# Six instead of four slots for the streamed activations, and all resident loads on one queue, in a fused attention and MLP kernel

## What is computed

```python
xn = layernorm(x)                                    # over the last axis, no gain or bias
w_masked = weight * block_mask(mask)                 # [4096, 4096], a block counts if its sum > 0
s = einsum('bsk,nk->bsn', xn, w_masked)
g = einsum('th,ih->ti', xn, w_gate) * s_gate         # 11008 wide
u = einsum('th,ih->ti', xn, w_up) * s_up
h = silu(g) * u
o = einsum('ti,hi->th', h, w_down) * s_down          # back to 4096
out = x + s * silu(o)
```

## Time and profile before

| | |
|---|---|
| two timed runs | 4385.27 and 4656.97 us, median 4521.12 |
| the profiled execution | 4384.07 us |
| its span on the slowest core, core 3 | 4382.5 us |
| spans of the other cores | 4360.7 to 4380.1 us |
| PE busy | 4082.6 us (93%) |
| DVE, ACT, POOL busy | 692.5, 210.4, 238.7 us |
| DMA, mean of the span | 137 GB/s |
| gate and up matmuls, L507 | 2,406 us |
| down matmuls, L681 | 728.0 us on `hTr`, 585.0 us on `hTl` |

### The profile page before, as it was taken

The page is one execution under the profiler, slowest core; times in us unless marked ns, Lnnn a source line. Parts: engine busy times, 40 slices in busy tenths (PEclk is TensorE's granted clock), DMA queues, the critical chain, the costliest instruction groups (busy, mean ns, idle before and its releaser), DMA issues. The chain is left out here.

```text
span 4382.5 us, 43424 instructions; the slowest of 8 cores (4360.7 to 4382.5 us)
## 1 busy us (share of the span) xinstructions
PE 4082.6 (93%) x19043; PEld 1849.6 (42%) x19043; DVE 692.5 (16%) x572; ACT 210.4 (5%) x265; POOL 238.7 (5%) x384
## 2 busy tenths in 40 slices
PE   1199998999999999999999999999499999999998
PEld 1144443444444444444444444444244444444443
DVE  4577631000000000000000000000000000000000
ACT  4100000000000000000000000000000000000000
POOL 0000000000000000000000000000011111111110
PEclk8599999999999999999999999999799999999999
DMA  4699643444444444444444444443778888887885
GB/s 155 239 336 333 245 154 72 85 85 86 86 87 87 87 87 87 87 87 87 87 87 87 87 87 87 87 87 77 204 155 180 194 177 163 194 192 157 184 194 133
DMA packets 205544, 599.18 MB, mean 137 GB/s; under 512 B 13156, under 2 KB 101552, under 8 KB 174000
## 3 DMA queue, kind: packets, MB, share of 16 engines
q0 software_dynamic: 120256, 287.33, 37.8%
q1 hardware_dynamic: 59808, 246.67, 16.9%
q10 hardware_dynamic: 25296, 62.40, 4.0%
HBM read 810.79 MB, written 47.71 MB: 196 GB/s over the span
## 5 line engine op out<-in xcount | busy, mean ns | idle before, releaser
L507 PE MATMUL p_g<-xnT,wgb 128*128 128x512 bf16 x5504 | 1204.3, 380 | 19.9 <-DMA wub<-hwu 19.9
L507 PE MATMUL p_u<-xnT,wub 128*128 128x512 bf16 x5504 | 1202.0, 379 | 0.0
L507 PEld LDWEIGHTS p_g<-xnT,wgb 128*128 128x128 bf16 x5504 | 539.9, 98 | 670.4 <-issue 23.4
L507 PEld LDWEIGHTS p_u<-xnT,wub 128*128 128x128 bf16 x5504 | 537.7, 98 | 650.2
L681 PE MATMUL p_acc<-hTr,wdb 128*128 128x512 bf16 x3072 | 728.0, 381 | 40.4 <-DMA hTr<-hTd 24.7
L681 PE MATMUL p_acc<-hTl,wdb 128*128 128x512 bf16 x2432 | 585.0, 384 | 30.3 <-DMA hTl<-hTd 30.3
L681 PEld LDWEIGHTS p_acc<-hTr,wdb 128*128 128x128 bf16 x3072 | 301.1, 98 | 417.5 <-issue 63.3
L542 DVE TENSOR_SCALAR uss<-p_u,su_cols 128x512 f32<-128x512 f32 x172 | 121.2, 746 | 2162.7 <-PE p_u L507 2162.7
L374 PE MATMUL p_sT<-xnT,wtm 128*128 128x512 bf16 x2048 | 448.6, 381 | 6.3 <-DVE wtm L425 6.3
L681 PEld LDWEIGHTS p_acc<-hTl,wdb 128*128 128x128 bf16 x2432 | 240.4, 99 | 325.2 <-issue 44.8
L374 PEld LDWEIGHTS p_sT<-xnT,wtm 128*128 128x128 bf16 x2048 | 199.1, 98 | 244.4 <-issue 9.5
(11 more groups left out here) (44 smaller groups left out, 302.7 us busy)
## 6 DMA issues: line engine op xcount, KB each, us to landing
wgb<-hwg POOLq DMA_DIRECT2D x86, 1024.0 KB, 8.7
wub<-hwu POOLq DMA_DIRECT2D x86, 1024.0 KB, 13.5
wdb<-hwd POOLq DMA_DIRECT2D x168, 512.0 KB, 6.9
hTl<-hTd SPq DMA_DIRECT2D x152, 512.0 KB, 5.5
mk<-mask SPq DMA_DIRECT2D x32, 2048.0 KB, 14.4
wts<-hwt SPq DMA_DIRECT2D x32, 2048.0 KB, 13.6
hTd<-hTt ACTq DMA_DIRECT2D x86, 256.0 KB, 10.2
xTl<-xT SPq DMA_DIRECT2D x32, 512.0 KB, 8.4
```

The source lines that it names most:

```text
L507: ins = te.matmul(p_x[th][:, :], A, xnT[:, blk_h * T + th * 512: blk_h * T + th * 512 + 512], start=(blk_h == 0), stop=(blk_h == 31))
```

## The change

`hTl` gets six slots instead of four, with six semaphores, and everything that counts by `p % 4` counts by `p % 6`: pair p >= 6 waits for pair p - 6, and the first six pairs of a group wait for pairs 18, 13, 14, 15, 16 and 17 of the group before. SP now issues all six `hTr` loads, in the order r = 0 to 5, before its waits for the last stores and the first pair; ACT issues none. The order of the items, the place of the `xTl` loads after pair 2 and everything else stay.

```diff
-        sm_hT_ld, sm_wd = sem4("hT_ld"), sem4("wd")
+        sm_hT_ld = [sem(f"hT_ld{i}") for i in range(6)]
+        sm_wd = sem4("wd")
...
-            hTl = [sb4(f"hTl{i}", [128, 2048], BF16) for i in range(4)]
+            hTl = [sb4(f"hTl{i}", [128, 2048], BF16) for i in range(6)]
...
-            _cnt4 = [0, 0, 0, 0]
+            _cnt6 = [0] * 6
             for _g in range(8):
                 for _p in range(NPAIR):
-                    _cnt4[_p % 4] += 1
-                    ht_use[(_g, _p)] = _cnt4[_p % 4]
+                    _cnt6[_p % 6] += 1
+                    ht_use[(_g, _p)] = _cnt6[_p % 6]
...
                 @blk.sync
                 def _(sy):
-                    for r in (0, 2, 4):
+                    for r in range(6):
                         sy.wait_ge(sm_hT_st[0], 16 * (4 * r + 4))
                         sy.wait_ge(sm_hT_st[1], 16 * (4 * r + 4))
                         sy.dma_start(
...
                     for g in range(8):
                         for p in range(NPAIR):
-                            if p >= 4:
+                            if p >= 6:
                                 sy.wait_ge(p4t,
-                                           g * NIT + POS[48 + 2 * (p - 4) + 1] + 1)
+                                           g * NIT + POS[48 + 2 * (p - 6) + 1] + 1)
                             elif g >= 1:
-                                q = {0: 16, 1: 17, 2: 18, 3: 15}[p]
+                                q = {0: 18, 1: 13, 2: 14, 3: 15, 4: 16, 5: 17}[p]
                                 sy.wait_ge(p4t,
                                            (g - 1) * NIT + POS[48 + 2 * q + 1] + 1)
                             sy.dma_start(
-                                hTl[p % 4][:, :].rearrange(
+                                hTl[p % 6][:, :].rearrange(
                                     "q (i t) -> q i t", i=2),
                                 d_hTd[48 + 2 * p:48 + 2 * p + 2, :, :].rearrange(
-                                    "i q t -> q i t")).then_inc(sm_hT_ld[p % 4], 16)
+                                    "i q t -> q i t")).then_inc(sm_hT_ld[p % 6], 16)
...
-                                te.wait_ge(sm_hT_ld[pr % 4],
+                                te.wait_ge(sm_hT_ld[pr % 6],
                                            16 * ht_use[(g, pr)])
-                                slot, sbase = hTl[pr % 4], (it % 2) * 1024
+                                slot, sbase = hTl[pr % 6], (it % 2) * 1024
...
                 @blk.scalar
                 def _(sc):
-                    for r in (1, 3, 5):
-                        sc.wait_ge(sm_hT_st[0], 16 * (4 * r + 4))
-                        sc.wait_ge(sm_hT_st[1], 16 * (4 * r + 4))
-                        sc.dma_start(
-                            hTr[:, r * 8192:(r + 1) * 8192].rearrange(
-                                "q (i t) -> q i t", i=8),
-                            d_hTd[8 * r:8 * r + 8, :, :].rearrange(
-                                "i q t -> q i t")).then_inc(sm_hr[r], 16)
```

## The result

| | before | changed |
|---|---|---|
| profiled execution, us | 4384.07 | 4402.55 |
| span of the slowest core | 4382.5 (core 3) | 4400.9 (core 2) |
| spans of the other cores | 4360.7 to 4380.1 | 4367.8 to 4397.1 |
| timed runs that the ratio compares | 4378.98 to 4400.09 (8 runs) | 4399.72 to 4402.55 (4 runs) |
| median of all timed runs | 4392.68 (14 runs) | 4766.82 (16 runs) |

The change costs 0.36%, about 16 us.

The account below looks back on a forecast made before the run. Data waits of TensorE were taken to lie only at the handover into the down stage, so deeper hTl slots gain nothing there. 4384.1 - 4 (handover) + 12.2 (lateness) + 1 (pair 3) + 2 (clock) = 4395 us, range 4374 to 4425.

Parts of the forecast that it names:

- The direction and the place: At position 1 of groups 1 to 7: seven PE waits for hTl, 0.5 to 3.3 us each; kernel slightly slower, 4395 us.
- +12.2 us of lateness: At the seven group ends: pair 0, issued only after position 84, lands late for position 1; ends 0 and 23.5 us.
- -4 us at the handover: Handover into the down stage: all hTr loads on SP's one queue move packets faster; ends 8.8 us less, 9.5 more.
- +1 us for pair 3: After group ends: pairs 1 and 2 in the burst delay pair 3, needed at position 14; ends 0 and 19.6 us.
- +2 us for the clock: At group ends: longer waits before position 1 shift or lengthen the slow-clock stretch; ends -2 and 8.4 us.
- The sum: Whole kernel: 4384.1 - 4 + 12.2 + 1 + 2 = 4395 us.
- The range: Whole kernel: 4374 to 4425 us, for an execution like the profiled one, not for the median.
- A: Group-end loads land in time and one queue is quicker at the handover: 4377 us; chance 0.25 together with D.
- B: At the handover one queue is no quicker or is slower: 4409 us, far case 4451; chance 0.13.
- C: At group ends pair 3 and the clock run to their ends, burst 1 MB larger: 4413 us; chance 0.12.
- D: Nothing moves: same handover bytes, group-end lateness hidden in the slow-clock stretch: 4384 us; chance 0.25 together with A.

## Why the prediction was right and wrong

**The direction and the place: right.** A small loss, in seven waits at position 1 of groups 1 to 7, because slot 0 comes free at position 84. The runs with one part each, and the run with the running slot numbers, bear out each link of this.

**+12.2 us of lateness: right.** 12.1 on core 2, 10.8 to 13.2 on the others that are late. The load took 9.0 us on average on core 2, 7.7 to 11.8, against 8.87 before. On the four cores that reach their ends first it is 0 to 1.8.

**-4 us at the handover: wrong, it is 0.** I took half of the difference between 155 packets per us on two queues and 197 that I worked out from two landings 1.3 us apart. The DMA queues of the changed kernel from 3112 to 3121 us, with one queue at work, against the earlier trace rows:

```profile
q1 hardware_dynamic: 1374, 2.77, 99.5%
```

1,374 packets in 9 us are 153 per us, against 155. The earlier trace rows had the reason already: the two queues together took 54.5 + 46.8 = 101.3% of the 16 engines' time, so there was nothing for one queue to gain. The step that failed is the 197, a rate made of two landings, not of packets counted in a stretch; why these came so close is not shown. The Trainium skill's rule ("DMA: Bandwidth & Descriptors", section "Issuing engines are not separate DMA queues") made this term 0; the 153 against 155 of this run and the 0.9996 of the one with the queue move alone agree with it.

**+1 us for pair 3: right here, and mis-sized as a risk.** On the late cores 0 to 2.1 us of the waits are at position 14. But the delay behind it was not the 2.8 us that I took: pair 3 is issued at the same point after the evictions' start, 12.65 us on core 2 and 12.64 before, and lands 15.4 to 19.9 us later, 17.0 on average, against 12.1 before. These 4.9 us are more than the slack of 3.0. The wait was small because PE came late for pair 0. With that gone it was 12.8 us on the slowest core and 17.6 on another, near the upper end (19.6) that I had kept for it.

**+2 us for the clock: too small on the slowest core.** The stretch from the evictions of group 0 to those of group 7, on core 3 before and on core 2 of the changed kernel (the first number after the stretch is its length, the second the busy time of PE):

```profile
3291.90:4367.06 1075.16, 1060.73 (x4816) 473.44 (x4816) 68.60 (x56) 33.13 (x57) 126.12 (x178) 0.99 0.83 178
3289.84:4385.70 1095.86, 1070.55 (x4816) 474.76 (x4816) 68.61 (x56) 33.12 (x57) 126.10 (x178) 0.97 0.82 175
```

Of the 20.7 us, 12.1 are waits for `hTl`, and 9.8 are the same 4,816 matmuls taking longer at the lower clock (mean granted clock 0.97 against 0.99); the waits for the evictions are 1.2 us shorter (14.2 against 15.4). So the clock term is 9.8, or 8.6 net of that. Two stretches of the end of group 1 (the granted clock is the third number from the end):

```profile
3451.00:3456.00 5.00, 0.37 (x1) 0.06 (x1) 4.58 (x5) 0.00 (x0) 0.00 (x0) 0.58 0.95 226
3456.00:3461.00 5.00, 4.76 (x12) 1.72 (x13) 2.19 (x2) 0.00 (x0) 0.00 (x0) 0.50 1.08 353
```

Before, the slow stretch was over with the 3 us of position 1; now PE sits idle through that stretch and the next one, with PE at work, is the slow one: 0.50, which is 1.2 GHz. I had named the upper end, 8.4 us, and took 2 because the idle time and the slow time might overlap. On this core they follow each other. That is not so everywhere: on cores 1, 5 and 7, with waits of 13.2, 10.9 and 10.8 us, PE is busy for 1061.2, 1065.0 and 1061.5 us in the same stretch, which is 0.5, 4.3 and 0.7 more than core 3 before. What decides between 0.5 and 9.8 is open.

**The sum.** 4384.1 + 0 + 12.1 + 8.6 = 4404.8, less 2.1 us because this core began its `down` block earlier (first `hTr` issue at 3084.3 against 3086.4) is 4402.7; measured 4402.55. I had 4395: the two misses, 4 and 6.6 us, go the same way.

**The range: wrong for the median of all runs.** 4374 to 4425 holds all four times that the ratio compares, and not the median of 4766.8. The step that failed is the sentence that the forecast is for an execution like the profiled one, "not for the median". One of the two times shown ahead was 4657 us, but times like it got no share of the chances, and 18 of the 30 were such: 4523 to 5247 us for twelve of the sixteen of the changed kernel. No term of the sum describes them, and what makes an execution one of them stays open here. Among the terms, the ones that were mis-sized are the handover (-4, measured 0) and the clock (+2, measured 8.6 net).

**The rivals.** A (one queue quicker, loads in time) is out: its first term is 0, and its second holds on the four early cores alone, which don't set the time. B is out: one queue is as quick as two. C was half right, in its clock term; its 4413 is also not its own two ends, which are 18.6 and 6.4 above the terms taken and give 4420. D is out.

## What to carry to other kernels

When a ring of buffers restarts in each round of a loop, look which slot the first load of a round takes: with a number of slots that doesn't divide the loads of a round, a fixed map can hand it the slot that is freed last (here 19 loads = 3 x 6 + 1, so slot 0 takes the first and the last load), while a running number keeps the full depth. A late load costs what lies between its landing and the position of its use, and behind it the next load at the edge is waiting: take the slack of each load in the order of use before you move one. Where a stage begins with more loads than it can start on, issue them in the order of use, in pieces as small as the first uses; that was worth 0.9% here, and moving one load to the front nothing.

## What was not expected of the hardware

- One hardware queue moved 2 KB packets at 153 per us (99.5% of the 16 engines' time), two together at 155 (101.3%).
- The cores of each pair of neighbours (0 and 1, 2 and 3, and so on) were 7 to 13 us apart at the end of group 0 of the changed kernel, one early and one late, and 28 to 31 us on cores 0 to 3 at the end of group 7, and a 512 KB load at the same point of the program took 5.7 to 8.0 us on the early cores and 7.5 to 11.8 on the late ones.
- Seven waits of 0.6 to 4.9 us at the group ends, where the granted clock falls, came with 9.8 us more of matmul time on core 2; on cores 1 and 7, with nearly the same waits, with 0.5 and 0.7.
